# Gate and up projections of twelve feed-forwards by one level of Strassen, in a fused macaron block

## What is computed

```python
up_gate = einsum('bsd,hd->bsh', x, W1)          # H = 2048, D = 512
up_lin  = einsum('bsd,hd->bsh', x, W3)
hidden  = fwht(silu(up_gate) * up_lin)          # Walsh-Hadamard transform over H
out     = einsum('bsh,dh->bsd', hidden, W2)

x = x + 0.5 * ffn(layernorm(x))
x = x + attention(layernorm(x))                 # ternary weights, chunks of 128 rows
x = x + 0.5 * ffn(layernorm(x))
```

## Time and profile before

| | |
|---|---|
| median of 3 runs | 2385.38 us (2384.45 to 2386.31) |
| the profiled execution | 2387.63 us, its span 2385.9 us |
| granted TensorE clock over the span | 0.999 |
| busy share of PE / DVE / ACT / POOL | 98% / 50% / 30% / 6% |
| DMA | 196.87 MB in 299460 packets, mean 83 GB/s |
| instructions on PE / DVE / ACT | 12851 / 2145 / 1196 |

### The profile page before, as it was taken

The page is one execution under the profiler, slowest core; times in us unless marked ns, Lnnn a source line. Parts: engine busy times, 40 slices in busy tenths (PEclk is TensorE's granted clock), DMA queues, the critical chain, the costliest instruction groups (busy, mean ns, idle before and its releaser), DMA issues.

```text
span 2385.9 us, 31855 instructions
## 1 busy us (share of the span) xinstructions
PE 2344.0 (98%) x12851; PEld 1121.7 (47%) x12851; DVE 1199.0 (50%) x2145; ACT 712.2 (30%) x1196; POOL 143.6 (6%) x102
## 2 busy tenths in 40 slices
PE   6999999999999999999999999999999999999999
PEld 3444445444444455444544454455445544544444
DVE  6576645554465445545455355534564455444312
ACT  5645333222232332223222332222233213322211
POOL 0090000000000000000000000000000000000000
PEclk9999999999999999999999999999999999999999
DMA  7947531242223322333142133411332223131210
GB/s 198 228 142 190 137 106 45 67 119 54 63 48 113 74 49 62 93 75 85 32 126 60 54 80 81 105 45 36 106 80 69 65 54 98 27 89 29 60 36 18
DMA packets 299460, 196.87 MB, mean 83 GB/s; under 512 B 231601, under 2 KB 256177, under 8 KB 295473
## 3 DMA queue, kind: packets, MB, share of 16 engines
q1 hardware_dynamic: 299024, 194.31, 31.4%
q10 hardware_dynamic: 288, 0.52, 0.1%
HBM read 84.68 MB, written 54.53 MB: 58 GB/s over the span
## 4 chain that ended last, share of the span: by engine, by line
PE 86%; DVE 3%; issue 3%; DMA 2%; POOL 2%; ACT 1%; SPq 1%; DVEq 0%; ACTq 0%; POOLq 0%
PE d_bank L1405 25%; PE l_bank L1385 24%; PE g_bank L1385 24%; PE a_bank L1440 5%; PE a_bank L1423 2%; PE a_bank L1499 2%; PE a_bank L1487 2%; PE a_bank L1451 1%; POOL work L714 1%; PE a_bank L1481 1%; POOL work L713 1%; DVE work L1122 1%; PE a_bank L1465 1%; DMA w1t<-kT 0%; DMA parts_dram<-q_parts 0%
## 5 line engine op out<-in xcount | busy, mean ns | idle before, releaser
L1405 PE MATMUL d_bank<-w2t,work 128*128 128x512 f16 x2940 | 673.7, 380 | 1.5 <-DVE work L1122 1.5
L1102 DVE SCALAR_TENSOR_TENSOR work<-l_bank,l_scale,work 128x512 f32<-128x512 f32 x256 | 191.7, 749 | 574.3 <-PE l_bank L1385 573.9
L1405 PEld LDWEIGHTS d_bank<-w2t,work 128*128 128x128 f16 x2940 | 285.1, 98 | 335.4 <-issue 4.3
L1385 PE MATMUL g_bank<-xt,w1t 128*128 128x512 f16 x1536 | 354.1, 380 | 4.7 <-DMA w1t<-q_parts 1.9
L1385 PE MATMUL l_bank<-xt,w3t 128*128 128x512 f16 x1536 | 352.4, 379 | 1.7 <-DVE work L1102 1.3
L831 ACT ACTIVATE work<-g_bank,g_scale 128x512 f32<-128x512 f32 x256 | 175.4, 685 | 503.5 <-PE g_bank L1385 497.1
L1385 PE MATMUL l_bank<-work,w3t 128*128 128x512 f16 x1344 | 308.4, 379 | 0.2 <-DVE work L1102 0.2
L1385 PE MATMUL g_bank<-work,w1t 128*128 128x512 f16 x1344 | 308.3, 379 | 0.0
L850 ACT CAST work<-work 128x512 f16<-128x512 f32 x232 | 143.3, 618 | 520.7 <-DVE work L1102 519.2
L1385 PEld LDWEIGHTS g_bank<-xt,w1t 128*128 128x128 f16 x1536 | 147.6, 98 | 181.0 <-issue 4.7
L1385 PEld LDWEIGHTS l_bank<-xt,w3t 128*128 128x128 f16 x1536 | 147.6, 98 | 175.7 <-issue 1.8
(11 more groups left out here) (216 smaller groups left out, 1699.6 us busy)
## 6 DMA issues: line engine op xcount, KB each, us to landing
work<-parts_dram SPq DMA_DIRECT2D x192, 128.0 KB, 2.8
x_dram<-work SPq DMA_DIRECT2D x16, 1024.0 KB, 4.6
work<-x_dram SPq DMA_DIRECT2D x11, 1024.0 KB, 7.1
parts_dram<-q_parts SPq DMA_DIRECT2D x32, 256.0 KB, 2.0
parts_dram<-k_parts SPq DMA_DIRECT2D x32, 256.0 KB, 2.2
norm_dram<-cent SPq DMA_DIRECT2D x32, 256.0 KB, 2.0
w2t<-in_L_ffn_W_dram SPq DMA_DIRECT2D x30, 256.0 KB, 3.4
xin<-in_L_attn_x_dram SPq DMA_DIRECT2D x7, 1024.0 KB, 7.6
```

Of the source, the lines that this page charges most:

```text
L1102: nc.vector.scalar_tensor_tensor(out=hfull, in0=l_bank[:], scalar=l_scale[:, j:j + 1], in1=gate, op0=ALU.mult, op1=ALU.mult).then_inc(hful ...
L1385: ins = nc.tensor.matmul(dst[:], wt[:, wp, k, P * j:P * (j + 1)], src[:, xp, k, :], start=(k == 0 and wp == xp), stop=(k == KT - 1 and wp ...
L1405: ins = nc.tensor.matmul(d_bank[t][:], parts[:, hp, P * t:P * (t + 1)], w2t[:, j, wp, :], start=(j == 0 and hp == wp), stop=(j == HT - 1 a ...
```

## The change

The first four feed-forwards stay. From the fifth on (n >= 4, `forked_feed_forward`) a feed-forward is four chunks of 12 slots. In a chunk each of W1 and W3 (`mat` 0 and 1) is multiplied by seven products of half size (half the rows of x, half of D, half of H): a product is 2 q x 2 k x 3 = 12 matmuls of 128x128 weights by 128x256. Five of the seven use sums of weight quarters. Those are built at the start in 32 pieces (`sload`, `smix`, `ssplit`, `sstore`: load, DVE sums, hi and lo parts, DMA transpose, store to `sum_dram`) and streamed from there in 256 KB units through a ring of eight homes. The seven sums of x (`umix`, `ulow`) take the place of prep and split for the norms of these feed-forwards; they are stored to `unit_dram` and come back by seven DMA transposes per feed-forward. Partial sums stay in PSUM: ACT copies the first product into `d_bank[0]` and the second to SBUF, DVE adds between products. "down" becomes four "part"s of 12 matmuls of 128x512 per chunk for the chunk before, into two banks, each followed by a DVE add to the residual rows.

Core of the diff (waits for buffers, loads of rows and the building of the sums cut):

```diff
+        PRODUCTS = (1, 5, 6, 2, 7, 3, 4)
+        SUMMED = (5, 6, 7, 3, 4)
+        REGIONS = (0, 3, 1, 2)
...
-                norm(end + 12 + TT, ("ffn2", b))
+                norm(end + 11 + TT, ("ffn2", b))
...
+                at = SUM_SLOT + 3 * i if i < EARLY_SUMS else LATER_SUM_SLOT + 3 * (i - EARLY_SUMS)
+                add(slots, at - 1, [("sload", i)])
+                add(slots, at, [("smix", i)])
+                add(slots, at + 1, [("ssplit", i)])
+                add(slots, at + 3, [("sstore", i)])
...
+        FIRST_NORM, PERIOD, GROUP_PERIOD, LAST_SHIFT = -13, 78, 12, 4
+        SUM_SLOT, LATER_SUM_SLOT = -14, 49
...
 (SP)
+                elif step == "ring":
...
+                        sp.wait_ge(p_done, product_at(used // 2, used % 2, SUMMED[k]))
...
+                    sp.dma_start(ring[arg % 8], sum_dram[mat, chunk % CHUNKS, unit].rearrange("p q k a h -> p (q k a h)")
+                                 ).then_inc(ring_landed[arg % 8], 16)
+                elif step == "operand":
...
+                        sp.wait_ge(p_done, product_at(chunk_of(nf, 0) - 1, 1, name))
...
+                    sp.dma_start_transpose(operand[u].rearrange("p (e t) -> p e t", t=P),
+                                           unit_dram[nf, unit].rearrange("p i e -> p (i e)")).then_inc(operand_landed[u], 16)
...
 (ACT)
+                elif step == "product":
+                    chunk, mat, name = arg
+                    if name == 1:
+                        act.wait_ge(p_done, product_at(chunk, mat, 1))
+                        if mat:
+                            act.wait_ge(s_gate, region_at(chunk, 2))
+                        elif chunk:
+                            act.wait_ge(s_hid, region_at(chunk - 1, 2))
...
+                            ins = nc.scalar.activation(d_bank[0][:, cols], g_bank[:, cols], ACT.Copy, scale=ratio[:, j, mat:mat + 1])
+                        ins.then_inc(forked, 1)
+                    elif name == 5:
...
+                        nc.scalar.copy(fifth(mat), l_bank[:]).then_inc(forked, 1)
+                    regions = {2: (0,), 3: (3, 1), 4: (2,)}.get(name, ())
+                    for region in regions:
+                        if mat == 0:
...
+                                ins = nc.scalar.activation(gate_s[region][:, cols], source(0, region)[:, cols], ACT.Silu, scale=scale)
+                            ins.then_inc(s_gate, 1)
+                        else:
...
+                            nc.scalar.copy(hid_s[:, region, 0, :], gate_s[region]).then_inc(s_hi, 1)
...
 (DVE)
+                    if name == 6:
...
+                        dve.wait_ge(forked, 2 * group + 2)
+                        nc.vector.tensor_tensor(d_bank[1][:], d_bank[0][:], fifth(mat), ALU.add).then_inc(shared, 1)
+                    elif name == 7:
...
+                        nc.vector.tensor_tensor(fifth(mat), d_bank[0][:], fifth(mat), ALU.add).then_inc(summed, 1)
+                    if mat == 1:
+                        for what, region in {2: (("linear", 0),), 3: (("linear", 3), ("low", 0), ("linear", 1)),
+                                             4: (("low", 3), ("linear", 2), ("low", 1))}.get(name, ()):
...
 (PE)
+                elif step == "product":
...
+                        pe.wait_ge(ring_landed[i % 8], 16 * (i // 8 + 2))
...
+                    elif name == 6:
+                        pe.wait_ge(forked, 2 * (2 * chunk + mat) + 1)
+                    elif name == 7:
+                        pe.wait_ge(shared, 2 * chunk + mat + 1)
+                    elif name == 4:
+                        pe.wait_ge(summed, 2 * chunk + mat + 1)
...
+                                ins = nc.tensor.matmul(dst[:, HALF_T * q:HALF_T * (q + 1)].rearrange("p (i t) -> p i t", i=2), weights,
+                                                       x_unit[:, :, xp, k, :], start=(name in (1, 5) and q == 0 and k == 0 and wp == xp),
+                                                       stop=(k == 1 and wp == 1), skip_group_check=True)
...
+                elif step == "part":
...
+                        pe.wait_ge(part_added, use - 1)
```

More of the change, by code:

```diff
@@ L267, in feed_forward, with chunk_of, product_at, region_at @@
                 steps += slots.get(base + 3 * j + 2, [])
[L268 to L269 removed]
+            return steps
+        PRODUCTS = (1, 5, 6, 2, 7, 3, 4)
+        SUMMED = (5, 6, 7, 3, 4)
+        REGIONS = (0, 3, 1, 2)
+        def chunk_of(n, c):
+            return CHUNKS * (n - FORKED) + c
+        def product_at(chunk, mat, name):
+            return 7 * (2 * chunk + mat) + PRODUCTS.index(name) + 1
+        def region_at(chunk, region):
+            return 4 * chunk + REGIONS.index(region) + 1
@@ L270, in feed_forward, with unit_norm @@
             if n == 2 * B - 1:
-                return steps + [("down", HT - 1)] + finish
-            return steps + ([("back", batch)] if which == "ffn2" else [])
+                steps += [("part", (chunk, t)) for t in range(TT)]
+            return steps
+        def unit_norm(key):
+            return key[0] in ("ffn1", "ffn2") and ORDER.index(key) >= FORKED
         def norm_steps(key):
+            if unit_norm(key):
+                return ([[("stat", key)]] + [[(step, (key, i))] for i in range(2) for step in ("uprep", "umix", "ulow")])
```

559 lines of the change are left out of this document (469 added, 90 removed).

## The result

| | before | after |
|---|---|---|
| median | 2385.85 us (4 runs) | 2667.93 us (2663.15 to 2672.91, 4 runs) |
| ratio | | 1.118, 95% interval 1.1155 to 1.1205 |
| span of the profiled execution | 2385.9 us | 2668.2 us |
| start of the fifth feed-forward | 611.85 us | 719.02 us |

What follows compares the result with a forecast made beforehand. PE, busy 98% of the span, was taken as the bound. From 2387.6 us, minus 113 (products), plus 167 (waits), 5 (sums) and 3 (transfers) gave 2449.6; with the median 2.3 lower, 2447 us, 2.6% slower, range 2325 to 2510.

Steps and rivals of the forecast that it cites:

- What the products save: W1 and W3 products of the forked feed-forwards: 1.31 us each, 2.36 us less a chunk, 113 us over 48 chunks.
- Bare chunk end: End of a chunk with empty slots: P6 starts 0.3 us late because ACT casts region 2 before the fork.
- Score 3: Chunks with score 3 in s10, batches 1, 3, 5: P6 1.75 us late, 10 times, 17.5 us.
- Kturn: Chunks with kturn in s11, batches 2, 4, 6: ACT's step delays the fork, P6 2.75 us late, eight times, 22 us.
- Sums of W: Beside the first four feed-forwards: 2.6 us of DVE a sum under 4 us of cover, costing 5 us (bounds 0 and 83).
- Norms: Norm steps in the forked chunks' slots delay P4, P6 and P7: four terms of 34, 48, 19 and 11.5 us.
- SP and DMA: Ring loads and transposes, mainly at feed-forward ends: nearly all covered, 3 us; 126 MB more, about 135 GB/s.
- Rival 1: At P6 and P7, queues absorb overlapping delays, leaving 48 x 1.0 us: faster, 2328 us, chance 0.27.
- Rival 2: PE waits for operands or ring units at 11 feed-forward ends and in chunks: +90, 2537 us, chance 0.07.
- Rival 3: Waits of 3 to 4 us lower PE's clock, each costing 1.7 us more: about 2485 us, chance 0.06.
- signs of being right: Products 1.31 us apart, P6 0.3 us late, PE waits of 150 us and more, P6's largest, DVE 60 to 68% busy.
- signs of being wrong: 256-column spacing outside 107 to 112 ns, PE's DMA waits above 20 us, clock below 0.97, waits under 105 us.

Runs made afterwards that it cites:

- DVE order: Changed kernel, with DVE multiplying regions 1 and 2 of W3 by their gates before subtracting the hi parts of regions 0 and 3: 2660.7 us.
- keep busy: Changed kernel plus 707 matmuls that compute nothing, ahead of P6 of mat 0 in 21 chunks where it waited for the fork: 2651.6 us.
- Early load: Changed kernel with the loads of the pieces of the sums of W issued four slots before their mix instead of one, a few excepted: 2618.9 us.
- short sums: Changed kernel with sum loads four slots ahead, and copies, sums and casts of all W pieces but two on an eighth of their columns: 2606.6 us.
- Short norms: Changed kernel with the forked feed-forwards' unit norms (normalised rows, sums, casts) made on an eighth of their columns, every instruction and wait kept: 2631.4 us.
- short plain norms: Most plain-norm work on an eighth of its columns, against a 2583.4 us kernel (earlier sum loads, linear 1 and 2 first, kturn mostly later, umix-ulow gap): 2552.6 us.
- casts on DVE: Norms' f16 casts moved from ACT to DVE, against a 2583.4 us kernel (earlier sum loads, linear 1 and 2 first, kturn mostly later, umix-ulow gap): 2555.8 us.
- late stores: Changed kernel with the first round of a unit norm's results stored in the second round, from the second round's contents: 2666.0 us.
- all out: Changed kernel with earlier sum loads, linear 1 and 2 first, kturn mostly later, unit norms and sums of W on an eighth of columns, first-round stores moved: 2534.3 us.
- Three edits of 49, 26 and 7 us: Changed kernel with sum loads four slots ahead, kturn one slot later, and linear 1 and 2 before the lows, all together: 2592.7 us.
- slots by parts: Changed kernel with slots 1 to 10 of a chunk moved beside the four parts, products following each other bare except for slots 0 and 11: 2801.5 us.
- fork first: Changed kernel with the steps of s11, s0 and s8 issued behind P6, so no slot stands between P1 and the shared add: 2738.0 us.

## Why the prediction was wrong

- **What the products save** (113 us): right. 1.31 us a product, also beside the slots.
- **Bare chunk end** (0.3 us): right to 0.01 us, and confirmed by the DVE order. **Score 3** (1.75): 1.4 to 1.6. **Kturn** (2.75): right in mechanism; 4.3 on average, as the longer waits carry the lower clock with them (2.7 in four of the eight once keep busy holds it up).
- **Sums of W** (5 us, bounds 0 and 83): the step that failed most, 107 us, outside its own bounds. The forecast priced the 2.6 us of DVE work a piece and its cover of 4 us. It did not price the wait in front of it: a load issued one slot (2.6 us of PE's work) ahead, where the earlier trace rows already had 3 us for a landing. Here the loads of the pieces land in 2.9 us (median, 2.5 to 7.5), and ACT waited for 23 of the 32 pieces, 120 us in all. The longest wait, 18.0 us, is only half landing: ACT was idle for 9.4 us before SP issued that pair of loads at all, and they had landed 8.5 us later. ACT's and DVE's queues stood behind it. Early load gave 53 us of this back, short sums some 15 more, with 36% of the sums' length gone. About 39 us stay unparted.
- **Norms** (112.5 us in the four terms): 204 us. The terms were sums of instruction lengths, with single waits between them. The step that failed is what they left out: that ACT and DVE wait for each other again and again inside these steps, ahead of the fork, and that a late product also runs at the lower clock. Short norms and short plain norms took 33 and 25 us away, with 58% and 64% of the length; at that rate the lengths are worth some 95 of the 204 us (an estimate), not far from what the forecast had. About 46 us are the lower clock (above). The rest is the order of two in-order queues that hand to each other, of which the casts on ACT ahead of the fork are a part (casts on DVE), the stores' landing a small one (late stores). The chunks "behind" a norm (10, 23), taken at 3.2 us, lost 10.8 and 11.5, because `prep` and `split` of the plain norm stand there, which the forecast costed only together. How the rest divides is not settled: 218 us stay in all out, a good part of it length that no run took away.
- **SP and DMA** (3 us): as a price about right for operands and ring, since only 7 us of PE's waits name `unit_dram`. With q and k moves (13.9 us) PE waits for DMAs 33 us in all, above the mark of 20; 13 of these are the wait in chunk 0, for which the forecast had no term. The bytes were put too low: 182 MB more and not 126, 142 GB/s on average and not 135.
- **The rivals.** Rival 1 (queues absorb) was wrong: the loss is 279 us, where it had 48. Three edits of 49, 26 and 7 us gave 75 together, so over the whole time the delays nearly add. Rival 2 had the kind of cause but not the place: transfers cost nothing at the feed-forward's ends and 53 us in front of the sums. Rival 3, the clock, was taken as an alternative to waits of the sum. It comes on top of them: 0.956, below the mark of 0.97, with 1.25 us on a late product (2.72 less 1.47), against the 1.7 us supposed. Its case stood in the trace of before: behind the 2.7 us wait of the earlier trace rows the next group of twelve was busy 4.44 us instead of 2.75.
- DVE is busy 58% (60 to 68 forecast). The mark was met nearly, and said nothing: the queues were late at a load that looks harmless. So it was with most signs of being right: spacing, late P6, waits over 150 us and their order all came as named, with a time that is 221 us off. Two of the signs of being wrong came as well, the DMA waits and the clock.
- The Trainium skill ("TensorE: Matmul & The Clock Gate", Back-to-back issue gap) had sustained spacings by which the products would have cost more than the full matmuls; the trace of after disagrees, with 109.2 ns a matmul of 256 columns (1.31 us for 12), about half of the 215.8 ns of 512.

## What to carry to other kernels

Price a step in an in-order queue by what it may have to wait for as well as by its length: here lengths were, by estimate, about half of the norms' cost, and loads issued one slot ahead cost 53 us where the forecast had 5 for the whole of the sums. And when a run shortens work to see what its length costs, measure how much shorter it became: an eighth of the columns left four tenths of the norms' time. A shorter matmul group shrinks the cover of everything beside it; if each dependency has only one group beside it, moving work past one only loads the next (slots by parts lost 133 us, fork first 70), and what helped was to take norm work off the engine that has the fork (28 us). Before such a change, count the dependencies with less than two groups of cover and the slots that can stand in front of them.

## What the runs showed of the hardware

- Behind 14 of the 19 longest fork waits (2.82 to 11.58 us) the product ran at 1.2 GHz: 2.72 us busy instead of 1.47 in most. Not always: one behind 3.43 us is busy 1.47; of four behind 2.62 and 2.63 us one is busy 1.47, the others 1.83 to 2.33. In before, twelve matmuls of 512 columns behind a wait of 2.68 us (and four short ones) were busy 4.44 us instead of 2.75. Useless matmuls in the gap raised the clock from 0.956 to 0.974, and the kernel became 16 us faster.
- ACT copies 512 columns from one PSUM bank into another, scaled by a factor from a table, in 0.65 us, and two halves of 256 columns in 0.81 us together. Out of PSUM into SBUF a plain copy takes 0.58 to 0.60 us, a Silu with a factor from a table 0.67 to 0.69. DVE's shared add, from one bank into another with an operand in SBUF, takes 0.70 us.
- Elementwise instructions shrink less than their columns: from 512 to 64 columns DVE's normalisation went from 542 to 311 ns, its subtraction from 689 to 221, ACT's cast from 615 to 243 (short norms).
- The DMA loads of the sum pieces landed in 2.9 us (median) and in 7.5 at most, where the DMA engines are 49 to 57% busy (240 to 719 us). A 256 KB store took 9.7 us to land among three moves of 1 MB, in before 10.2, where most such stores take 2.0.
